# Attention beside a mixture of experts on one core: routing steps spread over six rounds, then four rounds with two scattered tiles each

## The reference, cut to what matters

```
s   = attention(xn)            # 16 query heads on 4 key/value heads, head size 128, causal, rotary with a scale
y   = shared_experts(xn) + sum over the 2 chosen of 16 experts of weight * expert(xn)
out = x + s * silu(y)
```

## Time and profile before

| | us |
|---|---|
| median of 3 runs | 737.78 (737.41 to 739.9) |
| span of the profiled execution | 735.7 |
| what lies around the span, against the median | 2.1 |
| PE busy in the span | 659.1 (90%) |
| DVE, POOL, ACT busy | 581.6, 537.8, 442.3 |

### The profile page before, as it was taken

The page is one execution under the profiler, slowest core; times in us unless marked ns, Lnnn a source line. Parts: engine busy times, 40 slices in busy tenths (PEclk is TensorE's granted clock), DMA queues, the critical chain, the costliest instruction groups (busy, mean ns, idle before and its releaser), DMA issues.

```text
span 735.7 us, 17233 instructions
## 1 busy us (share of the span) xinstructions
PE 659.1 (90%) x4994; PEld 460.8 (63%) x4995; DVE 581.6 (79%) x1683; ACT 442.3 (60%) x1205; POOL 537.8 (73%) x588
## 2 busy tenths in 40 slices
PE   3678869789999999999999999999987899999992
PEld 1255546556766667676666766667665577767761
DVE  6988879789999999998999999999876344333378
ACT  3585636465657666575675657668584664555542
POOL 4677777978888887888877888888988993555510
PEclk9899989999999999999999999999998999999996
DMA  9491000500000000000000000000122564665772
GB/s 306 165 301 48 1 0 2 141 22 16 0 14 14 0 14 0 14 7 7 14 0 14 0 14 14 0 14 2 35 70 88 167 117 105 138 141 138 210 285 101
DMA packets 64952, 50.44 MB, mean 69 GB/s; under 512 B 35252, under 2 KB 58260, under 8 KB 64916
## 3 DMA queue, kind: packets, MB, share of 16 engines
q1 hardware_dynamic: 60804, 39.45, 19.3%
q0 software_dynamic: 3840, 10.52, 4.3%
q10 hardware_dynamic: 272, 0.02, 0.0%
HBM read 24.72 MB, written 18.96 MB: 59 GB/s over the span
## 4 chain that ended last, share of the span: by engine, by line
POOL 41%; issue 19%; PE 17%; DVE 13%; ACT 7%; DMA 2%; POOLq 0%; SPq 0%; DVEq 0%
POOL arena L539 16%; PE bank L1546 8%; POOL arena L533 8%; POOL arena L526 7%; PE bank L1576 6%; POOL xs_dram L586 4%; ACT arena L777 3%; POOL compare L582 2%; PE bank L1555 2%; DVE arena L1108 2%; POOL arena L563 1%; ACT arena L785 1%; DVE arena L1082 1%; DVE arena L1083 1%; DVE arena L1078 1%
## 5 line engine op out<-in xcount | busy, mean ns | idle before, releaser
L539 POOL TENSOR_TENSOR arena<-arena,rinv 128x128 f32<-128x128 f32 (+3 forms) x256 | 176.4, 720 | 83.5 <-DVE rinv L1102 83.4
L777 ACT ACTIVATE arena<-bank,nmax 128x512 f32<-128x512 f32 (+3 forms) x256 | 132.5, 535 | 64.6 <-DVE nmax L1096 64.6
L1096 DVE CUSTOM_DVE_ANT_0 bank<-bank,mask_b 128x512 f32<-128x512 f32 (+3 forms) x256 | 118.1, 516 | 14.2 <-issue 14.2
L1390 PE MATMUL bank<-arena 128*128 128x512 f16 (+7 forms) x768 | 116.4, 302 | 5.9 <-POOL arena L533 5.9
L785 ACT CAST arena<-bank 128x512 f16<-128x512 f32 (+1 forms) x192 | 93.3, 522 | 45.1 <-PE bank L1403 43.5
L1359 PE MATMUL bank<-xnT_hi,arena 128*128 (+1 forms) x320 | 111.0, 389 | 9.2 <-DVE arena L1083 4.7
L1419 PE MATMUL bank<-arena 128*128 128x512 f16 (+7 forms) x768 | 118.0, 305 | 0.0
L1403 PE MATMUL bank<-ident_f,arena 128*128 128x128 f32 x640 | 93.5, 277 | 25.5 <-DVE arena L1108 14.5
L1108 DVE TENSOR_TENSOR arena<-bank,arena 128x512 bf16<-128x512 f32 (+1 forms) x192 | 109.0, 595 | 3.9 <-ACT arena L785 1.8
L526 POOL TENSOR_TENSOR arena<-arena 128x512 f32<-128x512 f32 x77 | 98.6, 1281 | 2.5 <-DVE arena L1083 2.2
L1403 PEld LDWEIGHTS bank<-ident_f,arena 128*128 128x128 f32 x640 | 74.0, 142 | 38.9 <-DVE arena L1108 18.3
(11 more groups left out here) (147 smaller groups left out, 1158.9 us busy)
## 6 DMA issues: line engine op xcount, KB each, us to landing
xs_dram<-s_sb SPq DMA_DIRECT2D x4, 1548.0 KB, 14.4
stage<-w_gate_up SPq DMA_DIRECT2D x16, 352.0 KB
arena<-ys_dram SPq DMA_DIRECT2D x8, 512.0 KB, 6.5
stage<-w_down SPq DMA_DIRECT2D x16, 176.0 KB
stage<-wq SPq DMA_DIRECT2D x4, 512.0 KB, 8.0
stage<-wo SPq DMA_DIRECT2D x4, 512.0 KB, 6.5
stage<-x SPq DMA_DIRECT2D x1, 2048.0 KB, 10.6
out<-s_sb SPq DMA_DIRECT2D x8, 256.0 KB, 2.1
```

The costliest lines, as they stand in the source:

```text
L539: ins = pool.tensor_tensor(pr, pr, rinv[:, par, qt:qt + 1].to_broadcast([P, (qt + 1) * P]), ALU.mult)
L777: ins = act.activation(probs[par][:, P_AT[qt]:P_AT[qt] + n], score_bank[u][:, col:col + n], ACT.Exp, scale=-1.0, bias=nmax[:, par, qt:qt + ...
L1096: ins = dve.tensor_tensor_reduce(score_bank[u][:, col:col + n], score_bank[u][:, col:col + n], mask_b[:, S - n:S], -1.0, 3e38, ALU.add, AL ...
L1390: ins = pe.matmul(score_bank[u][:, col:col + n_k], qT[a][:, j * S + qt * P:j * S + (qt + 1) * P], kT[m][:, 0:n_k], start=(n == 0), stop=(n ...
```

## The change

Seven kinds of round become rounds numbered 0 to 5, then four `pair` rounds (6 to 9), then rounds 10 to 15 as before.

* x30, x31 and the router with its logits go from round 0 to round 1. ACT's normalising of batch 2 goes from ahead of round 0 into it, and that of batch 3 into round 1.
* Of the weight splits only the last moves, from round 2 to round 3.
* `route(0)` and `route(1)` go to round 2 (after j = 0 and j = 2), with `shift_logits`. `choose`, the exponential, `route(2)` and `select` go to round 3; `weigh`, `route(3)`, `rank` and `place(rd, 0)` to round 4; `tag`, `place(rd, 1)`, `slots` and `place(rd, 2)` to round 5.
* `place(rd, 0)` now stands behind `output_lo(rd, 1)` on DVE. It stood ahead of it.
* No tile is sent in rounds 2 to 5. Rounds 6 to 9 send tiles 0 to 7, the second of each pair with `set_out` after j = 2 on ACT, `rows_low` ahead of `divide(rd.head(GH), 0)` and `scatter` behind `rotate_lo("q2")` on POOL. Rounds 10 to 15 send the tiles that they sent before.

```diff
-ITEMS_FIRST = ["q0", "v", "x10", "q1", "x11", "x20", "k", "x21", "x30", "q2", "x31", "q3", "logit"]
-ITEMS_SECOND = ["q0", "v", "q1", "o0", "k", "o1", "rank", "q2", "o2", "q3", "o3"]
+ITEMS_FIRST = ["q0", "v", "x10", "q1", "x11", "x20", "k", "x21", "q2", "q3"]
+ITEMS_SECOND = ["q0", "v", "q1", "o0", "x30", "k", "o1", "x31", "q2", "o2", "q3", "o3", "logit"]
+ITEMS_RANK = ["q0", "v", "q1", "o0", "k", "o1", "rank", "q2", "o2", "q3", "o3"]
-X_AFTER = [[], ["x11"], ["x21", "x30"], ["x31"]]
+X_AFTER = [[], ["x11"], ["x21"]]
+X_SECOND = [[], ["x30"], ["x31"]]
+LOOP_FROM, PAIRS_END = 6, 10
+EARLY_ITEMS = [ITEMS_FIRST, ITEMS_SECOND, ITEMS_LOOP, ITEMS_LOOP, ITEMS_RANK, ITEMS_LOOP]
+WEIGHTS_AT = {(0, 0): 4, (0, 1): 5, (1, 0): 6, (1, 1): 7, (2, 0): 8, (3, 1): 9}
+WEIGHTS_BY = [4, 6, 8, 9, 10, 10]
+ROUTE_AT = {(2, 0): 0, (2, 2): 1, (3, 2): 2, (4, 1): 3}
-    def tile(self):
-        return None if self.early else self.i - 2
+    def tiles(self):
+        if self.early is not None or self.prologue or self.kind == "epilogue":
+            return []
+        return [self.i * 2 - 2 * LOOP_FROM, self.i * 2 - (2 * LOOP_FROM - 1)] if self.pair else [self.i - 2]
...
@@ gpsimd, round_ (of each j; select moves from ahead of j = 2) @@
+                    if j == 1 and tiles_:
+                        scatter()
+                    if rd.early == 3 and j == 0:
+                        choose()
+                    if (rd.early, j) in WEIGHTS_AT:
+                        weights_lo(WEIGHTS_AT[rd.early, j])
-                    if rd.second:
-                        (shift_logits, choose, weigh)[j]()
-                    if rd.third and j == 0:
+                    if rd.early == 2 and j == 1:
+                        shift_logits()
+                    if rd.early == 4 and j == 0:
+                        weigh()
+                    if rd.early == 5 and j == 0:
                         tag(rd)
-                    if rd.third and j == 2:
+                    if rd.early == 5 and j == 2:
                         slots()
                 if not rd.last:
                     rotate_lo("k", rd.rot("k"))
                     rotate_sum("q2", rd.item("q2"))
+                    if rd.pair:
+                        pool.wait_ge(rows_ready, tiles_[1] + 1)
+                        rows_low(tiles_[1])
                     divide(rd.head(GH), 0)
+                    if rd.pair:
+                        pool.wait_ge(rows_split, tiles_[1] + 1)
                     rotate_lo("q2", rd.rot("q2"))
+                    if rd.pair:
+                        scatter()
+                    if rd.early == 3:
+                        select()
...
-            scatter_tile(0)
-            with pool.Fori(3, NG - 2) as i:
-                round_(Round(i, "loop"))
+            round_(Round(LOOP_FROM, "pair"))
+            with pool.Fori(LOOP_FROM + 1, PAIRS_END) as i:
+                round_(Round(i, "pair"))
+            with pool.Fori(PAIRS_END, NG - 2) as i:
+                round_(Round(i))
...
@@ scalar @@
-            normalise(2)
-                        if j == 0:
-                            normalise(3)
-                    if rd.early and j < 2:
-                        weights_hi(W_FIRST + 2 * rd.i + j)
+                    if rd.early == 1:
+                        x_items_hi(rd, X_SECOND[j])
+                    if rd.early in (0, 1) and j == 0:
+                        normalise(2 + rd.i)
+                    if (rd.early, j) in WEIGHTS_AT:
+                        weights_hi(WEIGHTS_AT[rd.early, j])
+                    if rd.pair and j == 2:
+                        set_out(rd.tiles()[1])
...
@@ vector, round_ @@
-                    if rd.second:
-                        if j < 2:
-                            route(j + 1)
-                        if j == 2:
-                            place(rd, 0)
-                    if rd.third and j == 1:
+                    if (rd.early, j) in ROUTE_AT:
+                        route(ROUTE_AT[rd.early, j])
+                    if rd.early == 5 and j == 1:
                         place(rd, 1)
                 output_lo(rd, 1)
+                if rd.early == 4:
+                    place(rd, 0)
                 rope("q2")
...
-                if rd.first:
+                if not rd.first:
+                    add_projection(rd, 3)
+                if rd.early == 1:
                     logits(rd)
-                    route(0)
-                else:
-                    add_projection(rd, 3)
-                if rd.second:
-                    route(3)
...
@@ tensor, round_ @@
-                        if rd.second and j == 2:
+                        if rd.early == 4 and j == 2:
                             rank(rd)
...
-                if rd.first:
+                if not rd.first:
+                    project_out(rd, 3)
+                if rd.early == 1:
                     router(rd)
-                else:
-                    project_out(rd, 3)
```

More of the change, by code:

```diff
@@ new lines, in __init__ @@
+    def __init__(self, i, kind="loop"):
+        self.i, self.kind = i, kind
+        self.first, self.last, self.prologue = kind == "first", kind == "last", kind == "prologue"
+        self.early = i if isinstance(i, int) and 0 <= i < LOOP_FROM else None
+        self.late = kind == "loop" and isinstance(i, int) and i == NG - 2
+        self.pair = kind == "pair"
+        self.items = {"prologue": ITEMS_PROLOGUE, "epilogue": ITEMS_EPILOGUE, "last": ITEMS_LAST}.get(kind, ITEMS_LOOP)
+        if self.early is not None:
+            self.items = EARLY_ITEMS[i]
+        loop, before_loop = len(ITEMS_LOOP), len(ITEMS_PROLOGUE) + sum(len(m) for m in EARLY_ITEMS)
+        if self.prologue:
+            start = self.base = 0
+        elif self.early is not None:
+            start = self.base = len(ITEMS_PROLOGUE) + sum(len(m) for m in EARLY_ITEMS[:i])
+        elif kind == "epilogue":
+            start = self.base = before_loop + loop * (NG - 1 - LOOP_FROM) + len(ITEMS_LAST)
+        else:
+            start, self.base = before_loop, before_loop + (i - LOOP_FROM) * loop
+        self.odd = start % 2
@@ L647, in round_ @@
             def round_(rd):
+                tiles_ = [] if rd.last else rd.tiles()
                 for j in range(GH - 1):
-                    if rd.second and j == 2:
-                        select()
                     if j == 0:
@@ L656, in round_ @@
                         shared_lo(0)
-                    if j == 1 and rd.tile() is not None and not rd.last:
-                        pool.wait_ge(rows_ready, rd.tile() + 1)
-                        rows_low(rd.tile())
+                    if j == 1 and tiles_:
+                        pool.wait_ge(rows_ready, tiles_[0] + 1)
+                        rows_low(tiles_[0])
                     divide(rd.head(j + 1), (j + 1) % 2)
@@ L662, in round_ @@
                         rotate_sum("k", rd.item("k"))
-                    if j == 1 and rd.tile() is not None and not rd.last:
-                        pool.wait_ge(rows_split, rd.tile() + 1)
+                    if j == 1 and tiles_:
+                        pool.wait_ge(rows_split, tiles_[0] + 1)
                     if j == 0:
@@ L668, in round_ @@
                         rotate_lo(f"q{j - 1}", rd.rot(f"q{j - 1}"))
-                    if rd.early and j < 2:
-                        weights_lo(W_FIRST + 2 * rd.i + j)
+                    if j == 1 and tiles_:
+                        scatter()
[3 more added lines that the diff above has]
+                        weights_lo(WEIGHTS_AT[rd.early, j])
                     if rd.last and j == 0:
@@ L674, in round_ @@
                         tile_order()
-                        scatter_tile(rd.tile())
+                        scatter_tile(rd.tiles()[0])
                     if rd.last and j == 2:
@@ L696, in round_ @@
                         pool.memset(fill[:, :, D + 1], 0.0).then_inc(zeroed, 1)
+                    if rd.early == 3:
+                        select()
             round_(Round(0, "first"))
-            round_(Round(1, "second"))
-            round_(Round(2, "third"))
-            scatter_tile(0)
-            with pool.Fori(3, NG - 2) as i:
-                round_(Round(i, "loop"))
-            round_(Round(NG - 2, "loop"))
+            for n in range(1, LOOP_FROM):
+                round_(Round(n))
+            round_(Round(LOOP_FROM, "pair"))
[3 more added lines that the diff above has]
+                round_(Round(i))
+            round_(Round(NG - 2))
             round_(Round(NG - 1, "last"))
@@ L836, in round_ @@
                     h, par = rd.head(j + 1), (j + 1) % 2
-                    if rd.second and j == 1:
+                    if rd.early == 3 and j == 0:
                         act.wait_ge(rt_shift, 1)
@@ L854, in round_ @@
                             expert_hi_part(0)
-                        if rd.tile() is not None:
-                            set_out(rd.tile())
+                        if rd.tiles():
```

(51 more changed lines are left out.)

5 lines of the change are left out of this document (1 added, 4 removed).

## The result

The changed kernel takes 742.77 us (median of 15 runs) against 740.25 us for the kernel before in the same rounds. The ratio is 1.0033, with an interval from 1.002 to 1.0045, that is 1.5 to 3.3 us slower. On a second chip it was 742.18 against 738.65 us, 1.0037 (1.0025 to 1.005). Forecast were +2.0 us and 739.8 us, in a range of 734.5 to 743.5 us. The absolute time lies 3 us higher, near the upper end of that range, mostly because the kernel before, run more often, had a median of 740.25 and not 737.78.

The account below looks back on a forecast made before the run. Rounds 4 to 13 were taken as bound by PE; the terms -0.7 - 6.2 - 0.5 - 2.4 + 3.9 + 4.15 + 3.8 gave +2.0 us on the 735.7 span, with 2.1 around it 739.8 us, range 734.5 to 743.5.

Parts of the forecast that it names:

- Start and round 1: Rounds 0 and 1: round 0 ends 0.7 us sooner, round 1 takes 37.5 us against 43.67, 6.2 us less.
- The memset's wait: Start of round 1: DVE's first row maximum stays behind POOL's memset, moves only 0.7 us; first head 1.9 us over steady.
- The term for round 1: Round 1: 31.5 + 1.9 + 1.4 + 2.0 + 0.7 = 37.5 us, against 43.67.
- Round 2: Round 2: router adds 2.7 us, route(0) 1.6, route(1) 1.2, head 11 gives 0.3 back; 36.7 against 37.19 us.
- Round 3: Round 3: choose, the last weight split and select cost nothing; 31.5 against 33.95 us, 2.4 less.
- Round 4: Round 4: route(3) 1.0 us over, place(rd, 0) delays PE's o2 by 2.9; 3.9 us over in sum.
- Round 5: Round 5: place(rd, 1) costs 1.1 us, slots with place(rd, 2) 3.05; together 4.15 us over.
- The pairs: Pair rounds: scatter ahead of the second head's divide starts it 2.18 us late, losing 0.96 us each; 3.8 us for four.
- The pairs are free: Rival, chance 0.12: ACT and DVE reorder around the late divide, so the pairs cost nothing; 736.0 us.
- The spread: Rival, chance 0.18: PE's lead or DVE's idle time covers routing in rounds 2, 4, 5 except slots and router; at most 7.8 off.
- The second `set_out`: Rival, chance 0.1: it comes late behind its scatter, or DVE has less room; 0.5 to 1 us more per pair, 743.
- The clock falls in round 4: Rival, chance 0.15: PE's stops in round 4 bring one 6.8 us half-clock stretch, some 2.5 us net; 742.3 us.

## Why the prediction came out right

**Bound, and where to look.** PE bound the steady rounds, and rounds 11 to 14 came out as before to 0.02 us. Of the change in rounds 0 to 14, all but 0.1 us happened in rounds 0 to 5 and 7 to 10.

**Start and round 1.** Round 0 got 0.5 us shorter, not 0.7, with a half clock in it; in the eight later profiles of the changed kernel and its variants whose round 0 has none it took 35.8 us. The memset's wait came as described: DVE's maximum began 4.23 us behind the reciprocal, against 4.22 before, and the experiment that moved the memset got 2.2 us back, which leaves the first head no longer than a steady one. The term for round 1 was 0.8 too large: ACT's two jobs ahead of the exponentials cost 1.1 (9.17 against a steady 8.07), not 1.4, and moving the normalising alone took all of it away. The next head took 8.64, so 1.7 over, not 2.0, and the last 0.5, not 0.7.

**Round 2.** The router's wait was 1.05 us, the number worked out, and its head came out 2.85 over for 2.7. `route(0)` and `route(1)` cost 1.2 and 0.8 us and not 1.6 and 1.2. 36.28 against 36.7.

**Round 3.** 31.27: the cover held for `choose`, `select` and the last split.

**Round 4.** The mechanism (place, the bank two items on, PE's o2) is the one measured, and PE's wait of 2.4 us is as forecast. The size was off by 0.9, and that is two errors: the fall of the clock, some 1.7 us, was left out, while `route(3)` cost 0.6 and not 1.0 (head 18 took 7.56 against 6.97), and `place` about 2.5 and not 2.9 (the last head took 4.2 over, the clock's part included).

**Round 5.** `slots` cost 2.74 us again, and 37.04 against 35.7. The step that failed is the assumption that this stop keeps the clock whole as it did in round 2 before. It stood 2.76 us there with the clock at 1.00, in the one profile of that kernel, and 2.74 here with the clock falling. That cost 1.1 us: the last head took 15.29 us here and 14.15 there. `place(rd, 1)` cost 1.3 us for 1.1. The clock fell behind both stops in the first profile and in each of the six later ones that have both.

**The pairs.** The mechanism is shown: moving the two issues took the cost away with all the work left in. 2.18 us was the lateness forecast and measured. The loss was 1.0 to 1.1 us a round and not 0.96, and 1.34 in the first, 4.5 in all and not 3.8. In round 8:

```profile
323.41 0.83 PE L1436 MATMUL bank<-ident_f,arena 128*128 128x128 f32 x5 [0.78 <-POOL arena L556]
```

PE takes up the second head's transposes 10.60 us into this round, against 9.66 into round 7 before: 0.94 later, all that was forecast. The rest comes inside the group. Its next work starts at 324.41, 1.00 us on, where 0.87 passed before (288.67 to 289.54); in round 7 it is 1.28. Why the transposes lasted longer wasn't followed.

**Rivals.** "The pairs are free" is refuted by round 7 alone. The spread didn't work as it says: rounds 4 and 5 lost what rounds 1 and 3 gained. The second `set_out` was in time; with the scatter moved its rounds cost nothing. "The clock falls in round 4", with a chance of 0.15, came true, and in round 5 too, with one stretch of 3.4 us in each instead of one of 6.8. What it took (some 2.8 us) was made up for in part: rounds 4 and 5 came out 2.3 us above the forecast and the pairs 0.7, rounds 1 to 3 1.5 us below it. In the profiles that doesn't cancel: rounds 0 to 10 add up to 3.8 us more than before in the first and to 5.1 in the second, and the sum had 2.05. It is the medians (2.5 and 3.5 us more) that come near the forecast. So the good total is in part luck, of errors of opposite sign.

The Trainium skill, "TensorE: Matmul & The Clock Gate", section "What's actually happening", says that the clock follows how busy the array was lately. The trace agrees for round 4: the clock fell behind 4.80 us in which PE was busy for 1.87, although no single wait in it exceeded 2.41 us. But it can't tell round 5 from round 2 before: in the 4.80 us that end with the stop PE was busy for 2.08 us here, and the clock fell, and for 2.06 there (141.2 to 146.0), and it didn't. What decides between them isn't shown.

## What to carry to other kernels

When work is spread over a pipeline that one engine bounds, its engine-time is rarely what it costs. What counts is what is queued behind each step on its in-order engine, and how long the bounding engine can stand the wait: the same two DMA issues cost 1.0 to 1.3 us a round behind a divide and 0.03 ahead of it. Look at buffers that are used in turn as well as at the engines: the item two places on waits for whatever was put in between (2.41 us for `place`, 1.05 us for the router). And remove stops of the bounding engine even when they look small: those of 2.41 and 2.74 us took 1.7 and 1.1 us more by the clock.

## What the runs showed of the hardware

An indirect DMA of 128 rows takes the issuing POOL 0.96 to 1.18 us (median 0.97), with 0.15 to 0.31 us idle ahead of it in rounds 6 and 7. Its transfer lands 2.5 us after the issue in the median of the kernel before (2.4 to 3.1), and 2.6 us in the changed one (2.5 to 3.6).

Inside the rounds the half clock came in stretches of 3.41 or 6.82 us. One of 3.4 us cost 1.1 us in round 5 and, by what was left over, 1.7 in round 4. Two stops of equal length (2.76 and 2.74 us) can differ in whether it follows. Nor does it take a long one: in the second profile of the changed kernel it fell at 111.0, behind the router, in 5.0 us of which PE was busy for 3.89, most of it with matmuls of 16 columns, and waited 1.05 us at the longest.
